# A Mamba and mixture-of-experts layer on one core: pair 0 of the first chunk copied by TensorE, and a new slot order

## The reference

```
xn  = layernorm(x)
# state-space branch
xr  = xn * rsqrt(mean(xn^2) + eps) * norm_w
xi, z = split(xr @ W_in)                      # 256 + 256
xc  = silu(causal_conv4(xi) + conv_b)
dt, B, C = split(xc @ W_x)                    # 64, 16, 16
dt  = softplus(dt @ W_dt + b_dt)              # per token and inner channel (256)
h_t = exp(dt * A) * h_(t-1) + dt * xc * B     # 256 channels x 16 states, along each sequence
y   = (sum over states of h * C + D_skip * xc) * silu(z)
s   = xn + y @ W_out
# expert branch
probs  = softmax(xn @ Wg)                     # 8 experts; the best 2, rescaled, give score
f      = sum over e of score_e * (relu(xn @ W1_e + b1_e) @ W2_e + b2_e)
out = x + s * silu(f)
```

## Time and profile before

| | us |
|---|---|
| median of 3 runs | 311.08 |
| the three runs | 312.34, 308.81, 311.08 |
| the profiled execution | 309.04 |
| its span, first to last instruction | 307.2 |

### The profile page before, as it was taken

One profiled execution on the slowest core, in us unless ns is written; L12 is line 12 of the kernel. 1 busy time (PEld: TensorE's weight loads), 2 busy tenths in 40 slices (PEclk: granted clock), 3 DMA queues, 4 the chain that ended last, 5 costly groups with the idle time before them and its releaser, 6 DMA issues. The chain is left out here.

```text
span 307.2 us, 4290 instructions
## 1 busy us (share of the span) xinstructions
PE 276.6 (90%) x1273; PEld 144.9 (47%) x1273; DVE 275.8 (90%) x317; ACT 224.3 (73%) x440; POOL 236.9 (77%) x184
## 2 busy tenths in 40 slices
PE   7996689989999999698999999799998799997992
PEld 5633234534726453136645554235762555561662
DVE  4778899949999999999999899999999999999993
ACT  1495496799994948999688686999666684696640
POOL 6327966359899975667999887668999688869893
PEclk9999979999999999999999999799999999999999
DMA  6938980006065830041470660050938600000002
GB/s 185 292 97 182 231 191 10 0 6 137 0 154 132 194 73 0 0 122 21 104 172 1 139 138 1 4 137 11 206 67 185 150 0 2 0 0 1 3 0 68
DMA packets 16630, 26.23 MB, mean 85 GB/s; under 512 B 4264, under 2 KB 9759, under 8 KB 16608
## 3 DMA queue, kind: packets, MB, share of 16 engines
q1 hardware_dynamic: 15794, 24.78, 34.5%
q0 software_dynamic: 384, 1.05, 1.5%
q10 hardware_dynamic: 430, 0.14, 0.2%
HBM read 8.00 MB, written 1.18 MB: 30 GB/s over the span
## 5 line engine op out<-in xcount | busy, mean ns | idle before, releaser
L390 POOL TENSOR_TENSOR hc<-hs,Ct 128x1024 f32<-128x1024 f32 x63 | 149.2, 2377 | 24.3 <-DVE hs L892 23.9
L892 DVE TENSOR_TENSOR_SCAN hs<-dec,pdbu 128x1024 f32<-128x1024 f32 x64 | 146.2, 2285 | 9.2 <-ACT dec L561 5.1
L561 ACT ACTIVATE dec<-rep,negA 128x512 f32<-128x512 f32 x126 | 86.9, 725 | 7.0 <-DMA rep<-dt_u 4.7
L879 DVE TENSOR_TENSOR pdbu<-rep,pB 128x1024 f32<-128x1024 f32 x63 | 77.3, 1228 | 5.5
L1119 PE MATMUL px<-xnT,w 128*128 128x512 f32 x128 | 64.6, 606 | 6.8 <-ACT xnT L624 2.8
L1125 PEld LDWEIGHTS px<-w,hT 128*128 128x128 f32 x512 | 60.8, 192 | 18.5 <-issue 9.4
L1125 PE MATMUL px<-w,hT 128*128 128x128 f32 x512 | 62.7, 277 | 3.0 <-ACT hT L690 3.0
L690 ACT ACTIVATE hT<-px,cols 128x512 f32<-128x512 f32 x64 | 43.5, 689 | 21.3 <-PE px L1125 10.7
L506 POOL TENSOR_TENSOR acc<-acc,ysc 128x512 f32<-128x512 f32 x29 | 37.6, 1297 | 17.6 <-ACT ysc L679 17.3
L679 ACT ACTIVATE ysc<-px,score 128x128 f32<-128x128 f32 x116 | 32.9, 371 | 14.6 <-PE px L1125 14.5
L1017 PE MATMUL py<-hc,rsel 128*32 128x512 f32 x256 | 39.2, 609 | 2.3 <-POOL hc L390 2.2
(11 more groups left out here) (155 smaller groups left out, 275.5 us busy)
## 6 DMA issues: line engine op xcount, KB each, us to landing
rep<-dt_u SPq DMA_DIRECT2D x120, 128.0 KB, 2.4
Ct<-c_rows SPq DMA_DIRECT2D x16, 256.0 KB, 5.0
w<-in_L_ffn_W SPq DMA_DIRECT2D x1, 1024.0 KB
rep<-dt_u POOLq DMA_DIRECT2D x8, 128.0 KB, 4.6
out<-xn SPq DMA_DIRECT2D x4, 256.0 KB, 2.5
x_sb<-in_L_attn_x SPq DMA_DIRECT2D x1, 768.0 KB, 5.7
win<-in_L_attn_W_in SPq DMA_DIRECT2D x1, 256.0 KB, 3.3
x_sb<-in_L_attn_x ACTq DMA_DIRECT2D x1, 128.0 KB, 2.6
```

Source lines behind the costliest of these rows:

```text
L390: eng.tensor_tensor(hc[:, n % HC_RING], hs[:, n % HS_RING], Ct[:, k % 2, j:j + 1, :].to_broadcast([P, 2, CH]), ALU.mult).then_inc(hc_last ...
L561: act.activation(dec[:, n % DEC_RING, i, :], rep[:, q, 0, :], ACT.Exp, scale=negA[:, q, j:j + 1])\
L879: dve.tensor_tensor(pdbu[:, :, :], rep[:, 2 * pair:2 * pair + 2, 1, :], pB[:, m % 2:m % 2 + 1, :].to_broadcast([P, 2, CH]), ALU.mult).then ...
L892: dve.tensor_tensor_scan(hs[:, n % HS_RING].rearrange("p b t -> p (b t)"), dec[:, n % DEC_RING].rearrange("p b t -> p (b t)"), pdbu[:, :, ...
```

## The change

- `PRE_JOBS` gets u0, u1 (dt*u of blocks 0 and 1) and e0, e1 (dt of them) ahead of m0a: four products with `csel` on PE, emptied by ACT into `rep`. The DMAs of pair 0 in chunk 0, on SP and on POOL, are gone; POOL keeps block 3. `wait_replicas` waits for e1's emptying for pair 0 of chunk 0; for all later chunks its counts are those of one copy less.
- `BUSY`: 3 idle products instead of 8 at the beginning, none instead of 4 ahead of the column transpose, none instead of 2 after "tr", 2 after "xc1" as before.
- The gate on DVE was five steps, with DVE waiting after each linked instruction; it is 15 steps now, one instruction each, and the wait stands ahead of the instruction that needs it.
- `set_far` is a step of its own (`"far"`), later than `times_dt`; the DMAs of copies wait for it.
- The second half of chunk 0's softplus on DVE moves from slot 0 to slot 1, behind scan 0.
- The last load of the Silu table on ACT, with the Silu of chunk 2's experts, moves from slot 124 to slot 96 + 36 = 132, behind the jobs.
- All tables are new. TABLE[1] to TABLE[3] are left out below, as are STEPS of the last chunks but for "far".

```
-PRE_JOBS = ["tr", "xc0", "xc1", "dt", "x0", "v0", "x1", "v1", "d0", "d1", "tn", "m0a"]
+PRE_JOBS = ["tr", "xc0", "xc1", "dt", "x0", "v0", "x1", "v1", "d0", "d1", "tn", "u0", "u1", "e0", "e1", "m0a"]
 EARLY = {
-    0: ["gl", "z1"], 1: ["z0", "m1a"], 3: ["m1b"], 6: ["m0b"], 8: ["gs"], 11: ["gb"],
+    0: ["gl", "z1", "m1b"], 2: ["m0b"], 3: ["z0"], 6: ["m1a"], 7: ["gs"], 11: ["gb"],
 }
 TABLE = [{
-    3: ["tr"], 6: ["z1"], 7: ["xc0", "z0"], 9: ["xc1"], 12: ["y0", "y1", "dt"], 13: ["m3a", "tn", "v0"],
-    15: ["gl", "v1"], 17: ["m2a", "m2b"], 18: ["m3b", "y2", "m4b"], 19: ["m4a", "y3"], 21: ["m5b", "y4"],
-    24: ["m5a"], 25: ["m6b", "m6a"], 27: ["y5"], 29: ["m7a", "y6", "m7b"], 32: ["gs", "y7"], 34: ["gb"], 36: ["o"],
+    3: ["tr"], 6: ["xc0", "z1"], 7: ["z0"], 9: ["xc1", "tn"], 13: ["y0", "dt", "y1", "v0"], 14: ["gl"], 15: ["m3b"],
+    16: ["m2b", "m2a"], 17: ["v1"], 18: ["m3a", "y2", "m4b"], 19: ["y3", "m5a"], 21: ["m5b", "m4a"],
+    23: ["y4", "m6a"], 25: ["m6b"], 27: ["y5", "m7a"], 28: ["m7b"], 29: ["y6", "gs"], 32: ["gb", "y7"], 40: ["o"],
...
 STEPS = [{
-    "silu": [11], "log1p": [13, 17], "correct": [18, 20], "sum_dt": [18, 18], "times_dt": [23, 29],
-    "scale_rows": [1], "normalise": [5], "gate": [18, 22, 25, 26, 29], "gate_e": [18], "gate_p": [20, 26, 27],
-    "gate_y": [19, 34],
+    "silu": [11], "log1p": [13, 17], "correct": [19, 20], "sum_dt": [17, 17], "times_dt": [20, 28],
+    "scale_rows": [0], "normalise": [7], "gate": [18, 18, 22, 23, 24, 25, 26, 27, 27, 27, 27, 27, 28, 28, 29],
+    "gate_e": [19], "gate_p": [19, 26, 27], "gate_y": [20, 35], "far": [21, 38],
...
+    "gate_e": [19], "gate_p": [19, 23, 30], "finish": [39], "gate_y": [18, 35], "far": [24, 37],
...
+    "gate_e": [19], "gate_p": [21, 24, 28], "finish": [19], "gate_y": [21, 35], "far": [25, 40],
 }, {
-    "gate_y": [21, 35],
+    "gate_y": [19, 40], "last_table": [36],
 }]
 START = {
-    "second": [0], "gate": [2, 3, 4, 4, 7], "gate_e": [0], "gate_p": [1, 3, 5],
+    "second": [1], "gate": [1, 2, 3, 3, 4, 4, 4, 4, 5, 5, 5, 5, 6, 6, 7], "gate_e": [0], "gate_p": [1, 5, 6],
 }
-BUSY = {"row": 8, "rows": 4, "tr": 2, "xc1": 2}
+BUSY = {"row": 3, "xc1": 2}
...
         def wait_replicas(eng, k, pair):
-            early = pair < HALF_PAIRS
-            eng.wait_ge(rep_in[pair], N_REP * (k + 1) - (N_REP // 2 if early else 0))
-            if k == 0 and early:
-                eng.wait_ge(rep_soft[pair], N_REP // 2)
+            if (k, pair) == (0, 0):
+                wait_emptied(eng, "e1", 0)
+            elif (k, pair) == (0, 1):
+                eng.wait_ge(rep_in[1], N_REP // 2)
+                eng.wait_ge(rep_soft, N_REP // 2)
+            else:
+                eng.wait_ge(rep_in[pair], N_REP * (k + (pair > 1)) + (N_REP // 2 if pair == 1 else 0))
...
-            for q in (3, 1):
-                replicas(pool, q, True)
+            replicas(pool, 3, True)
...
+                elif job in ("u0", "u1"):
+                    ins = act.activation(rep[:, int(job[1]), 1, :], src[:, :], ACT.Copy)
+                elif job in ("e0", "e1"):
+                    ins = act.activation(rep[:, int(job[1]), 0, :], src[:, :], ACT.Copy)
...
-                elif n == 2 * (UNITS - LEAD):
-                    act.preload_act_table_set("silu_and_others")
-                    silu_of_experts(CHUNKS - 2)
...
+                for _ in steps_at(n, "last_table"):
+                    act.preload_act_table_set("silu_and_others")
+                    silu_of_experts(CHUNKS - 2)
...
                 for i in range(TPC):
-                    last = dve.max(gv8[:, i, :], gp[:, i, :])
-                link(last)
-                yield
+                    ins = dve.max(gv8[:, i, :], gp[:, i, :])
+                    if i == TPC - 1:
+                        ins.then_inc(gate_step, 1)
+                    yield
+                dve.wait_ge(gate_step, done + 4)
+                dve.tensor_reduce(gs2[:, :], gv8[:, :, 0:2], AX.X, ALU.add).then_inc(gate_step, 1)
+                yield
...
                 dve.tensor_tensor(dt_u[:, b, 1, :], dt_u[:, b, 0, :], xc[:, k % 2, b], ALU.mult).then_inc(u_done, 1)
+
+            def set_far(k, b):
+
                 dve.wait_ge(u_done, DB * k + b + 1)
                 dve.memset(dt_u[:, b, 0, 0:CH:SEQ], FAR).then_inc(far_done, 1)
...
-            keep_busy(BUSY["rows"])
             pe.wait_ge(w_rows, 16 * N_ROWS)
...
+                elif job in ("u0", "u1"):
+                    pe.wait_ge(u_done, 1)
+                    last = pe.matmul(dst[:, :], copies(int(job[1])), dt_u[:, 0, 1, :], start=True, stop=True)
+                elif job in ("e0", "e1"):
+                    pe.wait_ge(far_done, 1)
+                    last = pe.matmul(dst[:, :], copies(int(job[1])), dt_u[:, 0, 0, :], start=True, stop=True)
```

More of the change, by code:

```diff
@@ new lines @@
+    "scale_rows": [0], "normalise": [7], "gate": [18, 18, 22, 23, 24, 25, 26, 27, 27, 27, 27, 27, 28, 28, 29],
+    "gate_e": [19], "gate_p": [19, 26, 27], "gate_y": [20, 35], "far": [21, 38],
+}, {
+    "silu": [10], "log1p": [15, 16], "correct": [18, 19], "sum_dt": [17, 19], "times_dt": [22, 31],
+    "scale_rows": [0], "normalise": [6], "gate": [18, 19, 21, 22, 23, 24, 24, 25, 25, 25, 25, 25, 25, 25, 26],
+    "gate_e": [19], "gate_p": [19, 23, 30], "finish": [39], "gate_y": [18, 35], "far": [24, 37],
+}, {
+    "silu": [10], "log1p": [14, 18], "correct": [17, 24], "sum_dt": [17, 23], "times_dt": [21, 27],
+    "scale_rows": [0], "normalise": [4], "gate": [21, 21, 23, 23, 25, 26, 27, 27, 27, 27, 27, 27, 27, 27, 28],
+    "gate_e": [19], "gate_p": [21, 24, 28], "finish": [19], "gate_y": [21, 35], "far": [25, 40],
@@ L90 @@
 AUX = 3
-BUSY = {"row": 8, "rows": 4, "tr": 2, "xc1": 2}
-OWN = {"o", "x0", "x1", "d0", "d1"} | {f"y{e}" for e in range(EXPERTS)} | {f"m{e}{b}" for e in range(EXPERTS) for b in "ab"}
+BUSY = {"row": 3, "xc1": 2}
+OWN = {"o"} | {f"{a}{i}" for a in "xdue" for i in range(2)} | {f"y{e}" for e in range(EXPERTS)} | {f"m{e}{b}" for e in range(EXPERTS) for b in "ab"}
 SLOTS = {n: [(j, 0) for j in EARLY[n]] for n in EARLY}
@@ L238, in mamba_moe @@
         c_out, c_in = sem("c_out"), [sem(f"c_in{i}") for i in range(2)]
-        rep_in, rep_soft = [sem(f"rep_in{i}") for i in range(PAIRS)], [sem(f"rep_soft{i}") for i in range(HALF_PAIRS)]
+        rep_in, rep_soft = [sem(f"rep_in{i}") for i in range(PAIRS)], sem("rep_soft")
         e_done, l_done = sem("e_done"), sem("l_done")
@@ L374, in _ @@
                 for pair in range(PAIRS):
-                    repeat_dt_u(k, pair ^ 1 if k == 0 and pair < HALF_PAIRS else pair)
+                    if (k, pair) != (0, 0):
+                        repeat_dt_u(k, pair)
             for k in range(CHUNKS):
@@ L555, in decay @@
                 k, j, pair = place(n)
-                if j == first_quad(k, pair) and i == 0:
+                if j == (1 if n < HALF_PAIRS * QUADS and pair == 0 else 0) and i == 0:
                     wait_replicas(act, k, pair)
@@ L811, in gate @@
             def gate(k):
-                n = [GATE_STEPS * k]
-                def link(ins):
-                    n[0] += 1
-                    ins.then_inc(gate_step, 1)
-                    dve.wait_ge(gate_step, n[0])
+                done = GATE_STEPS * k
                 src = bank_of("gl", k)[:, 0:TPC * EXPERTS].rearrange("p (t e) -> p t e", e=EXPERTS)
                 wide = [P, TPC, EXPERTS]
+                wait_filled(dve, "gl", k)
+                dve.tensor_reduce(gmx[:, :], src, AX.X, ALU.max).then_inc(gate_step, 1)
+                yield
                 order.append(("gl", k))
-                wait_filled(dve, "gl", k)
-                link(dve.tensor_reduce(gmx[:, :], src, AX.X, ALU.max))
+                dve.wait_ge(gate_step, done + 1)
                 dve.tensor_tensor(glc[:, :, :], src, gmx[:, :, None].to_broadcast(wide), ALU.subtract)\
@@ L828, in gate @@
                 dve.wait_ge(gate_exp, k + 1)
-                link(dve.tensor_reduce(gsm[:, :], gex[:, :, :], AX.X, ALU.add))
-                link(dve.reciprocal(gri[:, :], gsm[:, :]))
+                dve.tensor_reduce(gsm[:, :], gex[:, :, :], AX.X, ALU.add).then_inc(gate_step, 1)
+                yield
+                dve.wait_ge(gate_step, done + 2)
+                dve.reciprocal(gri[:, :], gsm[:, :]).then_inc(gate_step, 1)
                 yield
@@ L875, in times_B @@
                 dve.wait_ge(B_spread, m + 1)
-                if j == first_quad(k, pair):
+                if j == (1 if n < HALF_PAIRS * QUADS and pair == 0 else 0):
                     wait_replicas(dve, k, pair)
@@ L944, in _ @@
             times_dt(0, 0)
+            set_far(0, 0)
             gates = [gate(k) for k in range(CHUNKS)]
@@ L952, in _ @@
                     times_dt(0, 1)
+                    set_far(0, 1)
                 if n == 2 * UNITS - 1:
@@ L960, in _ @@
                     correction(k, b)
+                for k, b in steps_at(n, "far"):
+                    set_far(k, b)
```

31 lines of the change are left out of this document (14 added, 17 removed), and 22 rows, old and new, of the table TABLE.

## The result

| | before | after |
|---|---|---|
| median (range), us, 4 runs each on one chip | 311.71 (308.81 to 312.74) | 301.73 (301.62 to 301.87) |
| ratio after/before | | 0.9695 (0.9627 to 0.9762) |
| profiled execution, us | 309.04 | 301.87 |
| its span, us | 307.2 | 300.0 |
| mean granted clock | 0.988 | 0.998 |

The kernel is 3.1% faster, and its runs lie within 0.25 us of each other where those of before are spread over 4. The profiled executions differ by 7.17 us, as do the fastest of each (308.81 and 301.62, 7.2), the medians by 9.98: the other 2.8 us are the slower executions of before, whose cause no trace here shows. The granted clock is a reading to take with care: the profiler's column says 1.00 until its first recorded change of the clock, also for the opening stretch, whose rows show the lower level.

The account below looks back on a forecast made before the run. DVE's scan and product, 3.70 us a unit, were taken as the bound. Gains 5.3 + 1.7 = 7.0, less 1.0, gave 6.0: 309.04 became 303.0, plus half of 2.04 made 304.0 us, range 300 to 309.

Parts of the forecast that it names:

- I shift all of it by 2.0: Startup: fewer idle products bring everything up to unit 0's two products 2.0 us earlier, to 24.8; bounds 0.7 and 3.0.
- the rival built on it: Startup: fewer idle products leave PE at 1.2 GHz, losing the 2.0 us and 1.6 besides: 307.6 us; chance 8%.
- Units 0 to 4: First scans: softplus half behind scan 0, no late pair 0 DMAs; scan 4 at 45.2 instead of 47.83, 2.6 us for DVE.
- the rival that they would land at 32.6: Units 1 to 4: pair 1's copies land no earlier than now, gaining only 0.9 us there: 306 us; chance 15%.
- The stall at unit 8: Unit 8: Silu table 5.0 us earlier, no stall there, but 2.5 us of new stall ahead of unit 9.
- the prediction's 5.3: From unit 10 on: DVE 5.3 us ahead, carried by ACT's chain to the second correction; bounds 2.5 and 6.
- 1.0 off: Three later chunk borders: new tables cost ACT and PE something, 1.0 us taken off the gain.
- Gate steps, FAR, table load: Between scans: gate steps in handovers 0.9 us, later FAR memset 0.8, table load nothing; together 1.7, bounds 0.5 and 2.5.
- Add half: Forecast median: half of the 2.04 us between before's median and its profiled execution added, making 303.0 into 304.0 us.
- PE and ACT could follow: Rival near units 24 and 40: PE and ACT can't follow, DVE stalls for decays; at 5 us lag 314 us; chance 7%.
- Smaller stalls: Rival: DVE waits for hc or late expert evictions, 1.5 us in each of three chunks: 308.5 us; chance 15%.

Follow-up runs that it names:

- a_busy: Kernel after with the idle products as in the kernel before (8, 4, 2, 2): 305.53 us.
- b_again: Kernel before, unchanged, run and traced once more: 310.76 us, ratio 1.0054.
- b_pair0: Kernel before with only pair 0 of chunk 0 copied by TensorE instead of DMAs; old tables, idle products and gate: 306.46 us.
- a_gmx: Kernel after with gl's maximum of chunk 0 moved from slot 1 to slot 2, behind the product of unit 1: 300.91 us.
- a_slot12: Kernel after with y0, dt and y1 back in slot 12 of the first chunk, between the two decays of unit 8: 303.17 us.
- a_dma0: Kernel after with pair 0 of chunk 0 copied by DMAs again, without u0, u1, e0, e1: 305.79 us.
- a_lump: Kernel after with the gate in five steps again, linked instructions with a wait behind each: 307.28 us.

## Why the prediction came out as it did

The forecast was 304.0 us with a range of 300 to 309; measured were 301.73. Sign and mechanism held: the stall ahead of unit 8 went, and pair 0 on PE with the changed slot did it. The sum of gains over the profiled execution was put at 6.0 and is 7.17, and that it is so near is partly luck: the first ten units gave 3.7 where 5.3 stood, and the rest 3.5 where 1.7 - 1.0 = 0.7 stood.

**Startup: wrong in the trace.** The step "I shift all of it by 2.0" failed. PE reached the column transpose at 7.33 for 8.98, 1.65 us earlier where 2.1 were predicted, but the two products of unit 0 end at 26.64 instead of 26.83: 0.2 us. What was missed is what came behind the spread: from the column transpose to the end of xc1 the kernel before takes 5.86 us (8.98 to 14.84), the one after 7.62 (7.33 to 14.95), since x's transposes and first products now go through at the lower clock until about 12 us. The rule of the Trainium skill that the prediction weighed ("TensorE: Matmul & The Clock Gate", What's actually happening), that activity releases the throttle, points this way. The traces agree for the first 12 us, with the spread at 3.77 instead of 2.22 us; not for the rival built on it, that PE would stay slow for the whole start. The working also called the opening pace half of the later one, but its own rows, 0.237 and 0.145 us a record, differ by 1.6 times. And the traces with all idle products show the other side: in two of four (a_busy and b_again, not before and b_pair0) the clock fell back after them. By the medians fewer idle products are worth 3.8 us in the kernel after, by its trace 1.1, which is no more than the spread of scan 0 among traces with few idle products (26.44 to 27.59). So their worth in the start is not settled by these runs; one profile of before couldn't tell it either.

**Units 0 to 4: 1.8 us, not 2.6.** The order of events is as walked: the softplus's half behind scan 0, no wait of ACT for DMAs, pair 1's copies used at 31.72 (the rival that they would land at 32.6 is out). DVE came to scan 0 1.9 us later than forecast, at 26.77 for 24.9, but of these 1.9 only 0.8 are left at scan 4 (46.01 for 45.2). The wait for gl, which the walk did not have at this length, is more than that: without it a_gmx has scan 4 at 44.99.

**The stall at unit 8: right.** It is gone but for 0.28 us, and the new one ahead of scan 9 is 1.92 us where 2.5 were predicted, with 0.77 ahead of the second correction. Silu to the end of the plus-one takes 73.43 - 53.66 = 19.8 us, predicted 19.4. The Silu table itself came 3.5 us earlier, not 5.0: PE's xc1 ended at 51.2 for the 49.6 of the sum, mostly the late start handed on. By a_slot12 the changed slot is worth 1.1 to 1.4 us (trace without the start, median), by b_pair0 and a_dma0 pair 0 is worth 3 to 4. The lead at the second correction, the milestone of the prediction's 5.3, is 3.7 (it starts at 77.13 before and 73.46 after); the 1.5 us by which the Silu table came later than forecast are nearly all of the miss.

**Unit 10 on: where 3.7 became 3.4 and then 7.2.** A scan is a poor milestone when the order of the work between scans has changed. Both corrections of chunk 1 stand ahead of scan 10 in both kernels, but the first times_dt moved ahead of it: it runs at 74.20 in the kernel after, and before it stood behind scan 11. DVE's timeline of before:

```profile
71.00 1.95 DVE L853 SCALAR_TENSOR_TENSOR xv<-xv,ev 128x512 f32<-128x512 f32 x1
...
77.13 1.18 DVE L853 SCALAR_TENSOR_TENSOR xv<-xv,ev 128x512 f32<-128x512 f32 x1 [0.28 <-ACT xv L588]
...
84.38 0.80 DVE L860 TENSOR_TENSOR dt_u<-dt_u,xc 128x512 f32<-128x512 f32 x1
```

The rows also show that the kernel before had its corrections stretched beside GpSimd, to 1.95 and 1.18 us, where the kernel after has 0.67 and 0.82. The windows from scan 10 to scan 63, before and then after (columns as above):

```profile
78.23:294.54 216.31, 202.45 (x971) 105.49 (x970) 205.75 (x192) 168.03 (x341) 181.96 (x110) 0.99 0.32 72
```

```profile
74.80:287.35 212.55, 200.67 (x973) 105.00 (x972) 204.46 (x191) 167.30 (x339) 182.18 (x110) 1.00 0.32 73
```

The stretch is 3.76 us shorter: DVE is busy 1.29 less and idle 2.47 less (10.56 to 8.09). The busy time is not less work: DVE's records in the two windows add up to 209.4 and 210.3 us, but more of them overlap their neighbours, small gate steps in the handovers above all. Of the idle time 1.2 are waits, 1.7 us in three places before, 0.5 after, in the same two stretches:

```profile
DVE sz L901 <- PE py L1017: 0.8, 1, 0.8
DVE hs L892 <- ACT dec L561: 0.6, 1, 0.6
DVE xv L853 <- ACT xv L588: 0.3, 1, 0.3
```

```profile
DVE pdbu L890 <- PE pB L1012: 0.5, 1, 0.5
```

The other 2.5 us of the 3.76 are the times_dt that moved out of the stretch, about 0.6 (unit 11 to 12 took 4.44 us before, 0.74 over the pace, 0.13 of it FAR), and some 1.9 for gate steps that now run in handovers, memsets that no longer wait for their product, and whatever else differs: predicted 1.7, right in size, though this remainder was not measured piece by piece. The term that was wrong in sign is "1.0 off" for the later borders: the new tables took 1.2 us of waits away there.

**Gate steps, FAR, table load.** FAR 0.6 to 0.9 (predicted 0.8), the table load nothing (predicted nothing). The gate steps alone were measured only from scan 10 to 12 (0.46 us), since further on a_lump brought a stretched product and a clock drop with it.

**The median.** "Add half" of the 2.04 us was the wrong way round. The executions of before lie up to 4 us above its profiled one, those of after do not: their median is 0.14 below the profile. Without that term the forecast had been 303.0.

**The rivals.** PE and ACT could follow: no wait for a decay near units 24 and 40 is left, and of slower there is nothing. Smaller stalls did not add up to anything either.

## What to carry to other kernels

A copy by DMA that lands late can cost far from where it is waited for: here the waits of an engine that was not the bound, 2.2 and 2.4 us at 32 and 36 us, made 2 us of another's stall some 30 us later, through the order in which the engines' queues are written. Before an instruction is moved into a gap, look at what GpSimd runs in that gap: a product of two SBUF tensors on DVE that starts while one of GpSimd runs ended 0.55 us after it here, and being ready earlier can gain nothing or cost. And take more than one trace before a step of the startup is priced, since the clock of the first 13 us or so differed from run to run with the same code.
